# A cross-attention and mixture-of-experts kernel: head loads in three transfers, rank sums taken ahead, a gather that waits, and new orders on every engine

## The chip, the cores and the metric

One core of one Trainium2 chip runs the whole program. The metric is the device time of one execution in microseconds (us), median of the runs. The engines are TensorE (PE, with its weight loads PEld), VectorE (DVE), ScalarE (ACT), GpSimd (POOL) and SyncE (SP, which here only issues transfers). Each takes its own instructions strictly in order, and they meet through semaphores.

## What is computed

Tokens `x` are 4 batches of 256 rows of 256 features, 1024 tokens in all.

```python
def _L0_xattn_ref(teacher_logits, teacher_features, Wq, bq, Wk, bk):
    query = jnp.einsum('bnc,dc->bnd', teacher_features, Wq) + bq
    key = jnp.einsum('bnc,dc->bnd', teacher_features, Wk) + bk
    energy = jnp.einsum('bnd,bmd->bnm', query, key)
    attention = jax.nn.softmax(energy, axis=-1)
    return jnp.einsum('bln,bmn->blm', teacher_logits, attention)

def _L0_ffn_ref(inputs, gate_weight, wi, wo):
    logits = tokens @ gate_weight.T
    probs = jax.nn.softmax(logits, axis=-1)
    top1 = jnp.argmax(logits, axis=-1)
    mask = jax.nn.one_hot(top1, E)
    ranks = jnp.cumsum(mask, axis=0) - 1        # place of a token in its expert
    mask = mask * (ranks < C)                   # C = 160 places per expert
    ...
    dispatch = jnp.einsum('tec,th->ech', sec_mask, tokens)
    hmid = gelu(jnp.einsum('ech,ehi->eci', dispatch, wi))
    eout = jnp.einsum('eci,eih->ech', hmid, wo)
    return jnp.einsum('tec,ech->th', combine_weights, eout)

x = x + _L0_xattn_ref(_layernorm(x), ctx_1024, Wq, bq, Wk, bk)
x = x + _L0_ffn_ref(_layernorm(x), gate_weight, wi, wo)     # 8 experts, 256 -> 1024 -> 256
```

## The kernel before, in words

All matrices are float32. The order on each engine is written out by hand as a list of calls of small functions, one list per engine (PE from L876, DVE from L593, ACT from L409, POOL from L318, SP from L217); a number in brackets is a batch `b` (0 to 3), a tile of 128 tokens `n` (0 to 7) or an expert `e` (0 to 7).

**The front.** `q` and `k` (L787, L796) make queries and keys of the contexts, in three chunks (batch 0, batch 1, batches 2 and 3); the contexts come in three transfers on SP (`context`, L197), the small weights in two on ACT (L361, L362). `en` (L811) makes the energies of a batch, `mx` (L491) their negated maximum on DVE, `exp` (L380) the exponentials on ACT. Tokens stay unnormalised: `bn1`, `st1`, `veps1` (L470 to L483) take their mean and variance, `first_rstd` (L288, POOL) the reciprocal root, `shift` (L485) the product that `shifted_input` (L295, POOL) adds. `turn_by` (L500) scales an identity by the reciprocal of the exponentials' sums; `at` (L818) turns the attention with it and appends the gate's columns; `xm` (L830) multiplies the turned tokens by it, and gives the attended tokens and the gate's logits together. `gate_mean` (L805) and `gate` (L464) take the mean off the gate's weights.

**Routing.** `x1` (L515) makes the new tokens in `rows`, `bn2`, `st2`, `veps2` (L578 to L590) and `second_rstd` (L300, POOL) their statistics. `scaled`, `summed`, `largest`, `less`, `value`, `first`, `chosen` (L520 to L554) make from the logits of a pair of tiles a one-hot `mask` (L553). `forerunners` (L846) and `rk` (L858) count on PE, by small bf16 matmuls, how many earlier tokens went to each expert: for each pair anew in the same 16 columns of PSUM, with one sum per earlier tile. `ranks` and `place` (L556, L562) read the place as a float (for `pick`, L568, which makes the 0/1 matrix of expert 0) and as an integer (for the scatter). `expz` (L394) makes the gate's weight. `scatter` (L306, POOL) writes each tile's rows to a slot table in DRAM, `slots_dram`. Expert 0 doesn't wait for that: `disp` (L865) makes its inputs by matmul from `tok` (L401, ACT) and `onehot`; two copies (L690 on DVE, L437 on ACT) bring them to SBUF.

**The experts.** PE runs `mm1` (L928) and `mm2` (L952) expert by expert. The other experts' rows come back from the slot table once all eight scatters have landed: `got_one` (expert 1), `got_zero` (expert 0, for the end only), `got_main` (experts 2 to 7, 780 KB) and `rest` 0 and 1 (the places 128 to 159 of four experts each). SP issues them (L232 to L236) all but `rest` 0, which ACT issues (L446) behind two GELUs. `load_tile` (L692) normalises a tile on DVE, `dT` (L918) transposes it on PE: tiles 0 and 1 (`got_one`, `rest` 0) inside `mm2(0)`, tile 2 (the first of `got_main`) inside `mm1(1)`, tile 3 ahead of `mm1(2)`. Behind the gathers SP queues four output copies of `rows` (L238), two small gathers (L213) and the weights of experts 3 to 7.

## Time and profile before

| | |
|---|---|
| median of 3 runs | 111.39 us (111.3 to 111.6) |
| the profiled execution's own time | 112.25 us |
| its span | 110.5 us |
| PE busy | 102.0 us, 92% of the span |
| PEld, DVE, ACT, POOL busy | 89.8, 34.6, 31.5, 31.1 us |
| chain that ended last, by engine | PE 78%, DMA 6%, DVE 4%, ACT 4%, issue 3% |
| moved by DMA | 25.77 MB, mean 233 GB/s |

The span runs from the first instruction to the last, the own time has what lies around it. In a timeline, what stands in square brackets behind an instruction is how long its engine had been idle and what ended that. One float32 matmul stands in the trace as two records.

### The profile page before, as it was taken

Reading aid. Unit: us, or ns where it says so; the run is one execution under the profiler, and the core shown is the slowest. Engines: PE = TensorE matmul, PEld = TensorE weight load, DVE = VectorE, ACT = ScalarE, POOL = GpSimd, SP = SyncE. Lnnn points to the kernel's source line nnn. Section 1 sums busy time; section 2 is a strip of 40 time slices with the busy share of each in tenths; the row PEclk is TensorE's granted clock in tenths of the full one; section 3 lists DMA queues with packets and bytes.
Section 4 is the critical chain, followed back from the end, with each engine's and each line's share of the span. In section 5 each row is a group of like instructions: output and inputs, shape, how many; then the busy total and the mean of one; then the engine's idle time right before and its main releaser. Section 6 shows DMA issues by size and latency. Waiting matters only on the chain.

```text
span 110.5 us, 1990 instructions
## 1 busy us (share of the span) xinstructions
PE 102.0 (92%) x758; PEld 89.8 (81%) x758; DVE 34.6 (31%) x151; ACT 31.5 (29%) x81; POOL 31.1 (28%) x55
## 2 busy tenths in 40 slices
PE   5988999999799999999999999999999999999900
PEld 5565888678689989999999998669999999888800
DVE  0019899999930041800420400220020010012110
ACT  3247675367534302332031041002303204100000
POOL 5501388586775000030210210303002011031540
PEclk9999999999999999999999999999999999999995
DMA  2799999999973499999999999950001001001100
GB/s 76 225 336 371 352 296 421 427 415 414 423 278 120 122 279 371 304 309 411 428 424 415 427 421 424 427 190 16 0 0 41 6 0 47 0 0 46 56 3 3
DMA packets 7986, 25.77 MB, mean 233 GB/s; under 512 B 928, under 2 KB 4773, under 8 KB 5928
## 3 DMA queue, kind: packets, MB, share of 16 engines
q1 hardware_dynamic: 6664, 23.24, 56.3%
q0 software_dynamic: 880, 2.12, 5.2%
q10 hardware_dynamic: 432, 0.27, 0.9%
q8 instruction: 6, 0.10, 0.4%
q14 instruction: 4, 0.03, 0.1%
HBM read 21.14 MB, written 4.76 MB: 234 GB/s over the span
## 4 chain that ended last, share of the span: by engine, by line
PE 78%; DMA 6%; DVE 4%; ACT 4%; issue 3%; SPq 1%; POOL 1%; ACTq 0%; DVEq 0%
PE ps L781 71%; DMA shared<-in_ctxT 6%; PE ps L871 3%; ACT shared L406 2%; PE ps L778 2%; PE ps L824 1%; ACT ez L398 1%; DVE rows L516 1%; POOL out L353 1%; SPq L199 1%; DVE nmax L493 1%; ACT attended L366 0%; DVE stats L580 0%; SPq L202 0%; DVE y_end L757 0%
## 5 line engine op out<-in xcount | busy, mean ns | idle before, releaser
L781 PE MATMUL ps<-wo_sb,shared 128*32 128x128 f32 (+2 forms) x320 | 36.6, 337 | 0.0
L781 PE MATMUL ps<-shared,wi_sb 128*128 128x160 f32 x256 | 36.3, 299 | 0.3 <-issue 0.3
L781 PEld LDWEIGHTS ps<-shared,wi_sb 128*128 128x128 f32 x256 | 35.1, 190 | 0.6 <-issue 0.4
L781 PEld LDWEIGHTS ps<-wo_sb,shared 128*32 128x32 f32 (+1 forms) x320 | 29.4, 142 | 5.1 <-issue 1.0
L448 ACT ACTIVATE shared<-ps 128x480 f32<-128x480 f32 (+1 forms) x24 | 12.6, 526 | 48.2 <-PE ps L781 48.2
L346 POOL DMA_INDIRECT out<-y,got x9 | 8.7, 971 | 59.3 <-DVE y L739 44.1
L739 DVE SCALAR_TENSOR_TENSOR y<-ps,share,got 128x256 f32<-128x256 f32 x9 | 4.4, 484 | 48.1 <-PE ps L781 24.7
L314 POOL DMA_INDIRECT slots_dram<-rows,slot x8 | 8.2, 1028 | 4.0 <-issue 1.4
L781 PE MATMUL ps<-attended,shared 128*128 128x272 f32 x32 | 8.4, 402 | 0.2 <-ACT attended L366 0.2
L781 PEld LDWEIGHTS ps<-attended,shared 128*128 128x128 f32 x32 | 5.7, 189 | 1.4 <-ACT attended L366 0.3
L871 PE MATMUL ps<-shared 128*128 128x160 f32 x32 | 5.3, 309 | 0.6 <-ACT shared L406 0.6
L781 PE MATMUL ps<-shared,small 128*128 128x256 f32 (+1 forms) x12 | 5.1, 542 | 0.8 <-DMA shared<-in_ctxT 0.7
L705 DVE TENSOR_SCALAR stok<-got 128x256 f32<-128x256 f32 x7 | 2.7, 415 | 9.0 <-DMA got<-slots_dram 9.0
L871 PEld LDWEIGHTS ps<-shared 128*128 128x128 f32 x32 | 4.6, 190 | 1.0 <-ACT shared L406 0.8
L472 DVE BATCH_NORM_STATS2 stats<-shared 128x6 f32<-128x256 f32 x8 | 3.0, 414 | 6.9 <-DMA shared<-in_x 6.9
L781 PEld LDWEIGHTS ps<-shared,small 128*128 128x128 f32 x12 | 2.4, 230 | 2.8 <-DMA shared<-in_ctxT 1.4
L824 PEld LDWEIGHTS ps<-turner,shared 128*128 128x128 f32 x32 | 4.2, 190 | 0.3
L824 PE MATMUL ps<-turner,shared 128*128 128x136 f32 x32 | 4.4, 279 | 0.0
L384 ACT ACTIVATE shared<-ps,nmax 128x256 f32<-128x256 f32 x8 | 3.7, 469 | 2.0 <-DVE nmax L493 2.0
L297 POOL TENSOR_SCALAR shared<-shared,shift 128x256 f32<-128x256 f32 x8 | 4.0, 508 | 0.4 <-DVE shift L488 0.4
L781 PE MATMUL ps<-shared 128*128 128x256 f32 x16 | 4.0, 384 | 0.0
L366 ACT ACTIVATE attended<-ps 128x264 f32<-128x264 f32 x8 | 3.0, 390 | 3.6 <-PE ps L824 3.5
(82 smaller groups left out, 77.4 us busy)
## 6 DMA issues: line engine op xcount, KB each, us to landing
wi_sb<-in_wi SPq DMA_DIRECT2D x8, 1024.0 KB, 16.6
wo_sb<-in_wo SPq DMA_DIRECT2D x8, 1024.0 KB, 16.7
slots_dram<-fill SPq DMA_DIRECT2D x1, 1300.0 KB, 13.1
shared<-in_x SPq DMA_DIRECT2D x2, 512.0 KB, 7.4
shared<-in_xT SPq DMA_DIRECT2D x2, 512.0 KB, 8.2
out<-rows SPq DMA_DIRECT2D x4, 256.0 KB, 5.4
got<-slots_dram SPq DMA_DIRECT2D x1, 780.0 KB, 6.6
got<-slots_dram SPq DMA_DIRECT2D x4, 130.0 KB, 2.4
```

Of the source, the lines that this page charges most:

```text
L297: nc.gpsimd.tensor_scalar(x_sb[:, n, :], x_sb[:, n, :], 1.0, shift1[:, n:n + 1], ALU.mult, ALU.add).then_inc(xs_done, 1)
L314: nc.gpsimd.indirect_dma_start(slots_dram, bass.IndirectOffsetOnAxis(ap=slot[:, n:n + 1], axis=0), rows[:, n, :], None, bounds_check=last_ ...
L346: nc.gpsimd.indirect_dma_start(out_rows, bass.IndirectOffsetOnAxis(ap=got[:, t, INDEX:INDEX + 1].bitcast(I32), axis=0), y[:, n % 2, :], No ...
L366: return nc.scalar.activation(dst, src, ACT.Copy)
L384: nc.scalar.activation(att[:, b, m, :], p_en[b][:, m * S:(m + 1) * S], ACT.Exp, bias=nmax[:, n:n + 1], accum_out=esum[:, n:n + 1]).then_in ...
L448: nc.scalar.activation(gelu[:, e % RING, a:z, :], p_h[j][:, 0:(z - a) * CAP], ACT.Gelu).then_inc(gelu_done, 1)
L472: nc.vector.bn_stats(stats[:, 0, n, :], x_sb[:, n, :]).then_inc(bn1_done, 1)
L705: nc.vector.tensor_scalar(stok[:, i % 2, :], row[:, 0:H], row[:, MEAN:MEAN + 1], row[:, RSTD:RSTD + 1], ALU.subtract, ALU.mult).then_inc(s ...
L739: nc.vector.scalar_tensor_tensor(y[:, n % 2, :], p_o[n % 2][:, 0:H], share[:, t:t + 1], got[:, t, 0:H], ALU.mult, ALU.add).then_inc(y_done, 1)
L781: return nc.tensor.matmul(dst, lhsT, rhs, start=(k == 0), stop=last)
L824: last = nc.tensor.matmul(p_at[c][:, E + m * P:E + m * P + HALF], att[:, b, m, c * P:(c + 1) * P], turner[:, b % 2, m * HALF:(m + 1) * HAL ...
L871: last = nc.tensor.matmul(p_disp[c], tok[:, n, c * P:(c + 1) * P], onehot[:, n, :], start=(n == 0), stop=(n == NT - 1))
```

## The change

1. **Head loads.** Contexts and small weights lie in one array `head` of 1298 columns and come in three SP transfers: Q's weights, both biases and context 0; K's weights, the gate and context 1; contexts 2 and 3. ACT issues none. `small` now lies inside the buffer `shared`.
2. **Gate mean.** One matmul of 16 columns for two of 8; DVE subtracts the two halves one after the other.
3. **First statistics.** `veps1` and `shift` go from DVE to POOL; tokens are shifted by a subtraction.
4. **Ranks.** All 64 columns (8 tiles by 8 experts) are started once by `rank_base`. After the mask of a pair, `rk` adds its own part and then each tile's sum to the columns of all later tiles. `forerunners` is gone.
5. **Places.** The float and the integer place are made by two calls, `place` and `row_numbers`; a scatter waits for one semaphore per pair, `row_ready`.
6. **Dispatch.** Tile 1 goes first and opens the sums; tile 0 is added on 128 columns. The first group of `mm1(0)` goes by halves: three matmuls on DVE's copy, then three on ACT's.
7. **Gathers.** SP waits for `got_one` and `rest` 0 to land before it issues `got_zero` and all that follows.
8. **Orders.** New lists on PE, DVE, ACT and POOL; `at` is called by half.

```diff
+W_Q, W_BQ, W_BK = 0, C, C + 1
+W_C0 = C + 2
+W_K = W_C0 + S
+W_G = W_K + C
+W_C1 = W_G + HC * E
+W_C2 = W_C1 + S
+W_ROW = W_C2 + 2 * S
+HEAD = [(0, W_K), (W_K, W_C2), (W_C2, W_ROW)]
...
-            context(0)
-            context(1)
+            head(0)
+            head(1)
             inputs(0)
-            context(2)
+            head(2)
...
             sp.wait_ge(scattered, 16 * NT)
             sp.dma_start(got[:, 1, :], by_rank[0:P, 1, :]).then_inc(got_one, 16)
+
+            sp.wait_ge(got_one, 16)
+            sp.wait_ge(rest_here[0], 16)
             sp.dma_start(got[:, 0, :], by_rank[0:P, 0, :]).then_inc(got_zero, 16)
             sp.dma_start(got[:, 2:E, :], by_rank[0:P, 2:E, :]).then_inc(got_main, 16)
...
             def first_rstd(i):
+                four = slice(4 * i, 4 * i + 4)
+                pool.wait_ge(st1_done, i + 1)
+                nc.gpsimd.tensor_scalar(mv[:, four, 1], mv[:, four, 1], EPS, None, ALU.add).then_inc(veps1_done, 1)
                 pool.wait_ge(veps1_done, i + 1)
...
+            def shift(i):
+                pool.wait_ge(rstd1_done, i + 1)
                 four = slice(4 * i, 4 * i + 4)
+                nc.gpsimd.tensor_tensor(shift1[:, four], mv[:, four, 0], rstd1[:, four],
+                                        ALU.mult).then_inc(shift1_done, 1)
...
             def second_rstd(b):
                 pool.wait_ge(veps2_done, b + 1)
+                if b == 0:
+                    pool.wait_ge(filled, 16)
...
             def scatter(n):
-                if n == 0:
-                    pool.wait_ge(slot_done, 1)
-                    pool.wait_ge(zs_done, 2)
-                    pool.wait_ge(filled, 16)
-                elif n % 2 == 0:
-                    pool.wait_ge(zs_done, n + 2)
-                    pool.wait_ge(slot_done, n // 2 + 1)
+
+                if n % 2 == 0:
+                    pool.wait_ge(row_ready[n // 2], 3)
...
-            act.dma_start(small[:, 0:W_FIRST], small_v[:, 0:W_FIRST]).then_inc(small_here[0], 16)
-            act.dma_start(small[:, W_FIRST:W_ROW], small_v[:, W_FIRST:W_ROW]).then_inc(small_here[1], 16)
...
             bn1(0)
-            mx(0)
             bn1(1)
             bn1(2)
+            mx(0)
             gate()
             bn1(3)
+            st1(0)
             recip(0)
             turn_by(0)
-            st1(0)
-            mx(1)
-            veps1(0)
             bn1(4)
             bn1(5)
+            mx(1)
...
-            def forerunners(b):
-
-                if b == 0:
-                    pe.wait_ge(exp_done, 6)
-                    pe.wait_ge(rank_consts, 4)
-                else:
+            def rank_base():
+
+                pe.wait_ge(exp_done, 6)
+                pe.wait_ge(rank_consts, 4)
+                nc.tensor.matmul(p_rank, one_row[:], expert_row[:], start=True, stop=False, skip_group_check=True)
+
+            def rk(b):
+
+
+                pe.wait_ge(mask_done, b + 1)
+                if b:
                     pe.wait_ge(rank_read, b)
-                nc.tensor.matmul(p_rank, one_row[:], expert_row[:], start=True, stop=False, skip_group_check=True)
-                for n in range(2 * b):
-                    nc.tensor.matmul(p_rank, eights[:], mask[:, n // 2, n % 2:n % 2 + 1, :].to_broadcast([P, 2, E]),
-                                     start=False, stop=False, skip_group_check=True)
...
+                last = nc.tensor.matmul(p_rank[:, 2 * b * E:2 * (b + 1) * E], before[:], mask[:, b, :, :], start=False,
+                                        stop=False, skip_group_check=True)
+                for t in range(2):
+                    n = 2 * b + t
+                    if n < NT - 1:
+                        last = nc.tensor.matmul(p_rank[:, (n + 1) * E:], eights[:],
+                                                mask[:, b, t:t + 1, :].to_broadcast([P, NT - 1 - n, E]), start=False,
+                                                stop=True, skip_group_check=True)
+                last.then_inc(rk_done, 1)
...
+                    if e == 0 and j == 0:
+
+
                         for c in range(HC):
-                            last = mm(p_h[j][:, (i - a) * CAP:(i - a + 1) * CAP], wi_sb[:, e, c, i * P:(i + 1) * P],
-                                      dispT[:, c, e, :], c, c == HC - 1)
+                            pe.wait_ge(disp_sb[c], 1)
+                            for i in range(a, z_):
...
```

What the new lists do to the instructions stands here at the three places that the prediction speaks of. DVE at its start, before (L472 is `bn1`, L493 `mx`, L466 `gate`, L498 and L510 the turner, L477 `st1`, L483 `veps1`, L488 `shift`):

```order
L472 BN_STATS stats<-shared 128x6
L493 TENSOR_REDUCE nmax<-ps 128x2
L472 BN_STATS stats<-shared 128x6 x2
L466 TENSOR_TENSOR idg<-small,ps 128x16
L472 BN_STATS stats<-shared 128x6
L498 RECIPROCAL erec<-esum 128x2
L510 TENSOR_SCALAR turner<-idg,erec 128x136 x2
L477 BN_AGGR mv<-stats 128x2 x4
L493 TENSOR_REDUCE nmax<-ps 128x2
L483 TENSOR_SCALAR mv<-mv 128x4
```

and now (L492 `bn1`, L502 `mx`, L484 and L487 `gate`, L497 `st1`, L507 and L519 the turner):

```order
L492 BN_STATS stats<-shared 128x6 x3
L502 TENSOR_REDUCE nmax<-ps 128x2
L484 TENSOR_TENSOR idg<-shared,ps 128x16
L487 TENSOR_TENSOR idg<-idg,ps 128x16
L492 BN_STATS stats<-shared 128x6
L497 BN_AGGR mv<-stats 128x2 x4
L507 RECIPROCAL erec<-esum 128x2
L519 TENSOR_SCALAR turner<-idg,erec 128x136 x2
L492 BN_STATS stats<-shared 128x6 x2
L502 TENSOR_REDUCE nmax<-ps 128x2
```

The first maximum moved behind two statistics, the first aggregation ahead of the turner, the second maximum behind two statistics of the second half. PE around the last two rank groups, before (L871 is `disp`, L853 to L862 the ranks):

```order
L871 MATMUL ps<-shared 128x160 x4
L853 MATMUL ps<-expert_row,one_row 128x16
L855 MATMUL ps<-mask,eights 128x16 x4
L861 MATMUL ps<-mask,before 128x16
L862 MATMUL ps<-mask,eights 128x8
L871 MATMUL ps<-shared 128x160 x4
L853 MATMUL ps<-expert_row,one_row 128x16
L855 MATMUL ps<-mask,eights 128x16 x6
L861 MATMUL ps<-mask,before 128x16
L862 MATMUL ps<-mask,eights 128x8
L871 MATMUL ps<-shared 128x160 x8
```

and now (L885 `disp`, L867 and L872 the ranks):

```order
L885 MATMUL ps<-shared 128x160 x2
L885 MATMUL ps<-shared 128x128 x2
L867 MATMUL ps<-mask,before 128x16
L872 MATMUL ps<-mask,eights 128x24
L872 MATMUL ps<-mask,eights 128x16
L885 MATMUL ps<-shared 128x160 x4
L867 MATMUL ps<-mask,before 128x16
L872 MATMUL ps<-mask,eights 128x8
L885 MATMUL ps<-shared 128x160 x8
```

The seven and nine small matmuls between dispatches became three and two. POOL at the scatters, before (L303 is `second_rstd`, L314 `scatter`):

```order
L314 DMA slots_dram<-rows,slot 1280x260
L303 TENSOR_TENSOR rows<-rows,minus_half 128x2
L314 DMA slots_dram<-rows,slot 1280x260
L303 TENSOR_TENSOR rows<-rows,minus_half 128x2
L314 DMA slots_dram<-rows,slot 1280x260 x2
L303 TENSOR_TENSOR rows<-rows,minus_half 128x2
L314 DMA slots_dram<-rows,slot 1280x260 x4
```

and now (L321, L328):

```order
L328 DMA slots_dram<-rows,slot 1280x260
L321 TENSOR_TENSOR rows<-rows,minus_half 128x2
L328 DMA slots_dram<-rows,slot 1280x260 x3
L321 TENSOR_TENSOR rows<-rows,minus_half 128x2 x2
L328 DMA slots_dram<-rows,slot 1280x260 x4
```

The third and the fourth scatter moved ahead of the third root.

## Rows read from the trace of the kernel before

**Rows 1.** Windows: span, length, busy of PE, PEld, DVE, ACT, POOL, clock, DMA, GB/s

```profile
15.10:20.40 5.30, 5.09 (x32) 4.05 (x30) 5.27 (x25) 3.41 (x15) 4.52 (x8) 1.00 1.02 397
20.40:28.70 8.30, 7.51 (x48) 6.24 (x49) 8.23 (x49) 4.93 (x18) 5.95 (x7) 1.00 1.02 419
28.70:32.40 3.70, 3.69 (x31) 3.33 (x31) 2.51 (x14) 1.30 (x6) 2.55 (x3) 1.00 0.87 355
...
40.00:60.00 20.00, 20.00 (x136) 19.18 (x134) 5.39 (x17) 4.74 (x9) 1.94 (x2) 1.00 1.02 374
```

**Rows 2.** Chain of waits, two pieces: start, length, what

```profile
2.16 6.44 DMA shared<-in_ctxT
...
32.73 7.17 PE ps L781 x44
```

**Rows 3.** Timeline, DVE: start, length, engine, line, operation, out<-in, count, idle before

```profile
7.99 0.43 DVE L472 BATCH_NORM_STATS2 stats<-shared 128x6 f32<-128x256 f32 x1 [6.93 <-DMA shared<-in_x]
8.33 0.67 DVE L493 TENSOR_REDUCE nmax<-ps 128x2 f32<-128x512 f32 x1
...
8.92 0.74 DVE L472 BATCH_NORM_STATS2 stats<-shared 128x6 f32<-128x256 f32 x2
```

**Rows 4.** Timeline, DVE and ACT at the hand-over to the experts

```profile
32.06 0.32 DVE L690 TENSOR_SCALAR shared<-ps 128x160 f32<-128x160 f32 x1 [0.98 <-PE ps L871]
...
32.28 0.30 ACT L437 ACTIVATE shared<-ps 128x160 f32<-128x160 f32 x1 [1.77 <-PE ps L871]
```

**Rows 5.** Timeline, the first gathered rows on ACT's queue, DVE and PE

```profile
36.36 0.57 ACTq L446 DMA_DIRECT2D rest<-slots_dram  x1
...
43.77 0.73 DVE L705 TENSOR_SCALAR stok<-got 128x256 f32<-128x256 f32 x2 [2.92 <-DMA got<-slots_dram]
...
44.30 0.38 PE L778 MATMUL ps<-idg,stok 128*128 128x128 f32 x2
```

**Rows 6.** Timeline, DVE: one add of eps and the instruction behind it

```profile
12.14 0.16 DVE L483 TENSOR_SCALAR mv<-mv 128x4 f32<-128x4 f32 x1
...
12.21 1.40 DVE L472 BATCH_NORM_STATS2 stats<-shared 128x6 f32<-128x256 f32 x4
```

**Rows 7.** Timeline, POOL: two small copies

```profile
9.80 0.33 POOL L285 COPY attended<-idg 128x16 f32<-128x16 f32 x2 [5.58 <-DVE idg L466]
```

**Rows 8.** Timeline, PE: six small sums of the last rank group, then dispatch

```profile
29.53 0.31 PE L855 MATMUL ps<-mask,eights 128*128 128x16 bf16 x6
...
29.75 2.50 PE L871 MATMUL ps<-shared 128*128 128x160 f32 x16
```

**Rows 9.** Timeline, the pick on DVE and the fourth dispatch on PE

```profile
28.02 0.54 DVE L575 TENSOR_SCALAR shared<-first_slots,slot_f,rows 128x160 f32<-128x160 f32 x1
...
28.71 0.78 PE L871 MATMUL ps<-shared 128*128 128x160 f32 x4 [0.61 <-ACT shared L406]
```

**Rows 10.** Timeline, POOL: last reciprocal root and fifth scatter

```profile
28.50 0.73 POOL L303 TENSOR_TENSOR rows<-rows,minus_half 128x2 f32<-128x2 f32 x1
...
29.99 1.04 POOL L314 DMA_INDIRECT slots_dram<-rows,slot  x1 [0.75 <-ACT ez L398]
```

**Rows 11.** DMA issues between 36.3 and 37.4: KB, us from issue to landing

```profile
got<-slots_dram SPq DMA_DIRECT2D x1, 130.0 KB, 2.1
rest<-slots_dram ACTq DMA_DIRECT2D x1, 130.0 KB, 2.8
...
got<-slots_dram SPq DMA_DIRECT2D x1, 780.0 KB, 6.6
```

**Rows 12.** Windows of half a microsecond, columns as in rows 1

```profile
37.50:38.00 0.50, 0.50 (x4) 0.44 (x3) 0.00 (x0) 0.29 (x1) 0.00 (x0) 1.00 0.80 243
...
43.50:44.00 0.50, 0.50 (x6) 0.50 (x5) 0.23 (x1) 0.00 (x0) 0.00 (x0) 1.00 1.20 416
```

**Rows 13.** DMA issue at 43.28, and PE's start of expert 3 in the timeline

```profile
wi_sb<-in_wi SPq DMA_DIRECT2D x1, 1024.0 KB, 8.5
...
54.07 4.51 PE L781 MATMUL ps<-shared,wi_sb 128*128 128x160 f32 x32
```

More of the change, by code:

```diff
@@ L89, in xattn_moe @@
         rows = sb("rows", [P, NT, ROW])
-        small = sb("small", [P, W_ROW])
         idg = sb("idg", [P, 2 * HALF])
@@ L196, in _, with head @@
         def _(sp):
-            def context(i):
-                a, z = CHUNKS[i]
-                sp.dma_start(ctxT[:, a:z, :], ctxT_v[a:z].rearrange("b c s -> c b s")).then_inc(ctx_here[i], 16)
+            def head(i):
+                a, z = HEAD[i]
+                sp.dma_start(small[:, a:z], head_v[:, a:z]).then_inc(head_here[i], 16)
             def inputs(i):
```

301 lines of the change are left out of this document (150 added, 151 removed).

## The prediction

> **What bounds the kernel now.** I read the windows by stage first. From 40 us on PE is busy in every microsecond: 20.00 of 20.00 between 40 and 60 [rows 1], and nothing in the change touches a matmul there. So time can come only from the front (up to the first expert matmul at 32.73 [rows 2]) or from a new wait for rows in the expert part. In the front, between 15.10 and 28.70, DVE is the fullest engine: 5.27 of 5.30 and 8.23 of 8.30, while PE idles 0.21 and 0.79; from 28.70 to 32.40 it is PE, 3.69 of 3.70 [rows 1]. The chain of waits agrees with the start: its first long piece is a context transfer that ends at 8.60 [rows 2]. DVE's own start is its wait for the tokens, 6.93 us up to 7.99 [rows 3].
>
> Second, the timeline at the hand-over. The first expert matmul runs at 32.73; the DVE copy it needs is done at 32.06 + 0.32 = 32.38, the ACT copy at 32.28 + 0.30 = 32.58 [rows 4]. Third, the same timeline at the first gathered rows. Scattering ends so that `rest` 0 is issued at 36.36, and `got_one` with it on SP. The six-expert gather `got_main` is read at 43.77, and the transposes that need it run at 44.30 [rows 5]. DVE's two tiles from it take 0.73 together [rows 5], so the first is there about 0.4 after the landing, near 44.2, and PE takes it at once. **There is next to no slack at this place**, and the change moves exactly this transfer.
>
> I set every later point against M, the first expert matmul (32.73). The transposes of `dT(2)` are due at 44.30 - 32.73 = M + 11.57.
>
> **The change, part by part.** The profiled execution took 112.25 with a span of 110.5; the median of the runs is 111.39, 0.86 lower. I apply the same difference in us to both.
>
> *Head transfers.* The same 649 KB or so go ahead of or beside the same token transfer, in three issues instead of five, and ACT issues none. Q and K may start some tenths earlier, but DVE waits for tokens until 7.99 [rows 3] whatever Q does. Cost 0. If the longer descriptors brought the tokens earlier, all of the DVE-bound front would follow; the nearest row gives no number, and I allow -0.3 to +0.3.
>
> *Order at the start of DVE.* The first maximum moves behind two more token statistics: in the profile it starts at 8.33, and the two statistics then take from 8.92 to 9.66 [rows 3]. The first exponentials and so the first turner come about 0.7 later. But DVE works on without a gap, so its sum is unchanged; the lateness reaches PE only at `at(0)` and again at `at(1)`. I take 0 and keep +0.4 as the bound (half of 0.7 and a little).
>
> *DVE work.* Two adds of eps and two shifts leave DVE. Such an add lasts 0.16 in its row, but the next instruction starts 0.07 later, 12.14 to 12.21 [rows 6], so four save 0.28. The gate gets a second subtraction that waits for the first: 0.15. Net -0.1. POOL gets the four; two small copies there took 0.33 [rows 7], so 0.17 each. They sit in front of the shifted tokens, which `x1` reads some microseconds on; hidden, and 0.2 if not.
>
> *Ranks.* 24 small matmuls become 12. Six took 0.31 [rows 8], so 0.05 each and 0.6 in all. Most of it falls where DVE sets the pace and is worth nothing. The last group does count, because PE is full after it: it has nine matmuls before and two after. Seven at 0.05 would be 0.35, but the six sums start at 29.53 and the dispatch already at 29.75 [rows 8], so they run partly into each other: I take -0.15. The first dispatch drops 32 of 160 columns: 2.50 / 16 = 0.156 per pass [rows 8], times 0.2, times four passes = 0.12, all before the third dispatch, where PE waits anyway. 0.
>
> *Stall at the fourth dispatch.* PE idled 0.61 before 28.71 [rows 9]. The profile names an ACT instruction, but the pick on DVE ended at 28.02 + 0.54 = 28.56, just before it; DVE is what is late. In the new order this pick comes after even more work of the third pair, so the stall moves to the third rank group or the third dispatch rather than going. I count -0.15 of it; the end that reaches furthest is all of PE's idle time up to there, 1.0 [rows 1]. **Front together: -0.4**, between +0.4 and -1.1.
>
> *Hand-over.* The first group of expert 0 now starts after DVE's copy alone and meets ACT's after three matmuls. Gain 32.58 - 32.38 = **-0.2**; between 0 and -0.25.
>
> *Scatter.* The third and fourth scatter go ahead of the third reciprocal root, and the last two roots run together. The last root ran at 28.50, behind a scatter, and the fifth scatter started at 29.99 [rows 10]. The other scatters follow with nothing to wait for, so the end moves with that start, about 0.5 earlier: as much as PE moves. No cost, and none gained, since `rest` 0 is issued by ACT behind its second GELU, at M + 3.6 as before [rows 5].
>
> *The new wait on SP.* `got_zero`, `got_main`, `rest` 1, the output copies and ten weight transfers now queue behind the landing of `got_one` and `rest` 0. These took 2.1 and 2.8 [rows 11]; with less beside them I take 2.4, so SP goes on at M + 6.0 and issues `got_main` at M + 6.45 (0.45 for issuing `got_zero`, a little under ACT's 0.57 [rows 5]). Before, it was issued 6.6 ahead of 43.77 [rows 5, 11], at 37.2 = M + 4.5: it moves back by 2. It took 6.6 to land [rows 11]. For what it takes now, the upper bound is 5.6: of the 390 KB that went ahead of it 260 KB are gone, and at the 243 GB/s of that stretch [rows 12] those took about 1.0. The lower bound is `got_one`'s 2.1 plus the other 650 KB at the best half microsecond near it, 416 GB/s [rows 12]: 1.6, together 3.7. I take the middle, 4.65: landing at M + 11.1, tile at M + 11.57, the very moment PE wants it. I put **+0.1** down, between 0 and +1.0 (with 6.6 unchanged it would be +1.9).
>
> Here the Trainium skill ("DMA: Bandwidth & Descriptors", Anatomy of one DMA, given for transfers from GpSimd) has a rule that does not fit the row: about 2.0 us fixed plus bytes over 436 GB/s per transfer, so 3.8 us for this one where the trace shows 6.6. By the page there would be no stall, and the sum would be 110.8; by the unchanged row it would be 112.7.
>
> The weights behind the wait: the first of them took 8.5 from 43.28, so it was there at 51.8, and it is needed at 54.07 [rows 13]. 2.3 of slack against 1.7 to 2 of delay: hidden, just; if it is not, a few tenths more. The first output scatter waits for the output copies, and has 6 us before anybody needs its buffer.
>
> **Sum:** -0.4 - 0.2 + 0.1 = -0.5: span 110.0, profiled 111.75, median 111.39 - 0.5 = **110.9**.
>
> **The rivals.**
>
> *A, the big gather is late (slower).* Place: `dT(2)`, the transposes at M + 11.57. Each microsecond that `got_main` takes beyond 4.65 is a microsecond of PE. The gain of 0.6 is eaten at 5.15, and the kernel is slower beyond what can be told at 5.5. For: the 6.6 of the row, and the output copies come just as close behind as before. Against: two of the three transfers ahead are gone. At 5.7 the stall is 1.1, and the time 111.39 - 0.6 + 1.1 = 111.9; up to 112.7. Chance 0.27.
>
> *B, the front gets longer.* The later first maximum is paid on PE, and POOL's extra work reaches `x1`: +0.4 for -0.4, the rest as above: 111.39 + 0.4 - 0.2 + 0.1 = 111.7. For: DVE's start is on the path. Against: DVE has work to fill every gap. Chance 0.13.
>
> *C, the orders do more than I credit.* PE's idle time up to 28.7 goes and the last rank group with it: -1.1 - 0.2 + 0.1 = -1.2, 110.2. For: `rk` no longer holds four or six sums between a mask and a dispatch. Against: DVE had 0.1 idle in 13.6 us, so somebody must wait for it. Chance 0.2. That the head transfers do nothing for the end is part of the forecast.
>
> **How the numbers follow.** Forecast 0.40, own range 110.5 to 111.3. A 0.27, B 0.13, C 0.20. The range 110.1 to 112.2 takes in C and most of A, and leaves out a tenth at each end. A measurement of this kernel can tell about 0.3% (0.33 us) from no change. Faster by more: three quarters of the forecast and nearly all of C, 0.49. Slower by more: most of A and over half of B, 0.29. Within: the rest, 0.22.
>
> **What would show it.** In the changed kernel's trace: the two first matmuls of expert 0 about 0.1 behind DVE's copy; DVE still above 95% from 15 us to the last pick; dispatch ending near 31.7; the six-expert gather issued near M + 6.4 and landing near M + 11.1. A gap of PE before the third transposed tile of over 0.5 us makes A right. A first expert matmul later than 32.7 makes B right, one before 31.7 C. The forecast is wrong in kind if a wait ends last that none of these names, such as a weight transfer before expert 3.

## The result, and the profile after

The change made the kernel slower. The median of six runs is 114.58 us (113.93 to 115.37), against 111.61 (111.3 to 112.32) for the kernel before on the same chip: ratio 1.026, with an interval of 1.0222 to 1.0297. Executions more than 1.5% above the fastest of a kernel, as most kernels have some, before too, are left out of the ratios but not of the medians. The profiled execution of after is the fastest of the six, 113.93 with a span of 112.1, and that of before (112.25, span 110.5) lies 0.64 above its median of 111.61. So the two profiles show 1.6 to 1.7 us of the loss, and the medians hold 1.3 more: 0.64 because before's profile lies above its median, 0.65 because after's lies below.

The windows by stage, the last of the front cut at 33.40, where PE now goes idle behind dispatch (32.40 in before) (columns as in [rows 1]):

```profile
15.10:20.40 5.30, 4.80 (x29) 3.51 (x27) 4.59 (x25) 1.80 (x6) 5.30 (x8) 1.00 1.03 394
20.40:28.70 8.30, 5.98 (x35) 5.18 (x35) 6.76 (x41) 4.05 (x16) 7.10 (x8) 1.00 1.01 419
28.70:33.40 4.70, 4.30 (x31) 3.85 (x31) 3.06 (x19) 2.84 (x12) 3.92 (x5) 1.00 0.84 337
40.00:60.00 20.00, 19.87 (x135) 18.82 (x134) 5.81 (x18) 4.30 (x8) 1.95 (x2) 1.00 0.94 326
```

Against [rows 1] two engines have changed places. DVE was full from 15.10 to 28.70 and is now busy 4.59 and 6.76. POOL is the full one: 5.30 of 5.30, then 7.10 of 8.30. The page's list of costly groups names the instruction that filled it. First the group in before, then in after (line, engine, operation, count, then busy us and mean ns):

```profile
L297 POOL TENSOR_SCALAR shared<-shared,shift 128x256 f32<-128x256 f32 x8 | 4.0, 508 | 0.4 <-DVE shift L488 0.4
```

```profile
L313 POOL TENSOR_SCALAR shared<-shared,shift 128x256 f32<-128x256 f32 x8 | 7.4, 935 | 0.1
```

The token shift was written as multiply by 1.0 and add, and is now a single subtraction. One operation instead of two, on the same 128x256 elements, takes 935 ns instead of 508. What that pushes back stands in three timelines of after, POOL, ACT and PE:

```profile
15.70 4.58 POOL L313 TENSOR_SCALAR shared<-shared,shift 128x256 f32<-128x256 f32 x5
20.25 0.72 POOL L321 TENSOR_TENSOR rows<-rows,minus_half 128x2 f32<-128x2 f32 x1
```

```profile
21.07 0.30 ACT L411 ACTIVATE ez<-below,rows 128x8 f32<-128x8 f32 x1 [2.03 <-POOL rows L321]
...
21.66 0.65 ACT L380 ACTIVATE attended<-ps 128x264 f32<-128x264 f32 x2
```

```profile
19.23 1.17 PE L834 MATMUL ps<-turner,shared 128*128 128x136 f32 x8
22.17 0.70 PE L834 MATMUL ps<-turner,shared 128*128 128x136 f32 x4 [1.78 <-ACT attended L380]
22.71 1.08 PE L793 MATMUL ps<-attended,shared 128*128 128x272 f32 x4
```

Five shifts fill POOL up to 20.25. Only then comes the reciprocal root of the first block (`second_rstd(0)`). ACT's exponential of that block's logits (`expz(0)`) waits for it until 21.07. The new order puts `expz(0)` ahead of the copies `at(2)`, which need nothing from POOL. PE needs those copies to free its PSUM for `at(3)`, and stands still for 1.78 us. Dispatch ends later by 0.9 us (30.67 + 2.50 = 33.17, against 29.75 + 2.50 = 32.25 in [rows 8]), and the first expert matmul comes later by 1.2. This is the hand-over, DVE, ACT and PE (before: [rows 2, 4]):

```profile
33.47 0.33 DVE L702 TENSOR_SCALAR shared<-ps 128x160 f32<-128x160 f32 x1 [1.43 <-PE ps L885]
34.19 0.30 ACT L454 ACTIVATE shared<-ps 128x160 f32<-128x160 f32 x1 [2.46 <-PE ps L885]
33.95 1.87 PE L956 MATMUL ps<-shared,wi_sb 128*128 128x160 f32 x12 [0.56 <-issue]
```

M is 33.95 where before had 32.73. The matmul follows DVE's copy by 0.15 (33.80 to 33.95), as meant; it is the copy that starts late, 0.30 behind the end of dispatch. One profile places M no better than within half a microsecond: d3 below, whose front is that of before, has it at 32.19.

The other part of the loss is the moved gather. The chain of waits now runs through it (before: [rows 5, 11]):

```profile
37.49 2.50 DMA rest<-slots_dram
...
40.44 4.88 DMA got<-slots_dram
...
45.34 0.42 DVE stok L717
...
45.81 0.44 PE ps L790 x2
```

`dT(2)` runs at 45.81 = M + 11.86, against M + 11.57: 0.3 us late. So the profiled loss is 1.22 in front of M and 0.29 up to `dT(2)` behind it.

### The profile page after: what moved, and what is told of

The parts are those of the page before. It is cut to its first block, busy times and chain, and to the rows that moved or that the text cites. A ratio compares the mean times of both kernels' runs of the same rounds, so it can differ in the third digit from the quotient of the medians.

```text
span 112.1 us, 1966 instructions
## 1 busy us (share of the span) xinstructions
PE 101.5 (91%) x744; PEld 89.4 (80%) x744; DVE 34.3 (31%) x148; ACT 31.1 (28%) x81; POOL 35.7 (32%) x59
## 4 chain that ended last, share of the span: by engine, by line
PE 63%; DMA 13%; POOL 7%; DVE 7%; issue 3%; SPq 2%; ACT 1%; ACTq 0%
PE ps L793 55%; DMA shared<-in_x 7%; POOL shared L313 5%; DMA got<-slots_dram 4%; PE ps L885 3%; DMA rest<-slots_dram 2%; PE ps L790 2%; PE ps L956 2%; DVE stats L492 1%; DVE rows L525 1%; SPq L204 1%; POOL rstd L303 1%; POOL out L369 1%; DVE stats L592 1%; POOL rows L321 1%
## 5 line engine op out<-in xcount | busy, mean ns | idle before, releaser
L793 PE MATMUL ps<-shared,wi_sb 128*128 128x160 f32 x244 | 34.6, 299 | 0.0
L793 PEld LDWEIGHTS ps<-shared,wi_sb 128*128 128x128 f32 x244 | 33.5, 190 | 0.2
L793 PE MATMUL ps<-shared 128*128 128x256 f32 (+1 forms) x28 | 9.2, 479 | 0.0
L328 POOL DMA_INDIRECT slots_dram<-rows,slot x8 | 8.2, 1023 | 2.0 <-issue 1.6
L793 PEld LDWEIGHTS ps<-shared 128*128 128x128 f32 x28 | 5.7, 226 | 2.3 <-issue 1.7
L313 POOL TENSOR_SCALAR shared<-shared,shift 128x256 f32<-128x256 f32 x8 | 7.4, 935 | 0.1
L885 PE MATMUL ps<-shared 128*128 128x160 f32 (+1 forms) x32 | 5.0, 306 | 0.3 <-DVE shared L587 0.3
L885 PEld LDWEIGHTS ps<-shared 128*128 128x128 f32 x32 | 4.5, 190 | 0.6 <-issue 0.3
L492 DVE BATCH_NORM_STATS2 stats<-shared 128x6 f32<-128x256 f32 x8 | 3.0, 417 | 6.3 <-DMA shared<-in_x 6.3
L525 DVE SCALAR_TENSOR_TENSOR rows<-ps,rstd,shared 128x256 f32<-128x256 f32 x8 | 3.8, 477 | 1.6 <-PE ps L793 1.2
L797 PE MATMUL ps<-warm_w 128*128 128x128 f32 x12 | 2.9, 410 | 1.1 <-DVE warm_w L470 1.1
```

What stands on the lines that cost most here:

```text
L313: nc.gpsimd.tensor_scalar(x_sb[:, n, :], x_sb[:, n, :], shift1[:, n:n + 1], None, ALU.subtract).then_inc(xs_done, 1)
L328: nc.gpsimd.indirect_dma_start(slots_dram, bass.IndirectOffsetOnAxis(ap=slot[:, n:n + 1], axis=0), rows[:, n, :], None, bounds_check=last_ ...
L492: nc.vector.bn_stats(stats[:, 0, n, :], x_sb[:, n, :]).then_inc(bn1_done, 1)
L525: nc.vector.scalar_tensor_tensor(halves(rows[:, n, 0:H]), halves(p_xm[n // 2 % 2][:, n % 2, 0:WIDE])[:, :, E:HALF], rstd1[:, n:n + 1], hal ...
L793: return nc.tensor.matmul(dst, lhsT, rhs, start=(k == 0), stop=last)
L797: nc.tensor.matmul(p_warm[:, 0:P], warm_w[:], warm_w[:], start=True, stop=True)
```

## The experiments

A ratio below is to the kernel before on the same chip. That kernel's median differed by chip: 112.09 beside the a and b runs, 110.8 beside c and d, 111.76 beside e and f. Only ratios are therefore compared across groups. The edits stand here in short: semaphore increments, function names and unchanged arguments are left out.

**Is it the form, and does the new wait cost?** Four kernels.

a1: after with the shift as two operations.

```
-  x_sb[:, n, :], shift1[:, n:n + 1], None, ALU.subtract
+  x_sb[:, n, :], 1.0, shift1[:, n:n + 1], ALU.mult, ALU.subtract
```

> The changed kernel with one edit: POOL's token shift is written with two operations again (times 1, minus the shift) instead of the single subtraction. Theory F (form of the instruction): one such POOL instruction took 935 ns in the changed kernel where the two-operation form took 508 ns; eight of them hold up the first second reciprocal root, which holds ACT through its exponentials of the gate, which stand ahead of the third attention copies, and PE idles 1.78 us. Then the instruction goes back to about 0.5 us, PE's idle time before the third attention falls under 0.4 us, the first expert matmul moves from 33.95 to 32.3 to 32.7, and the time falls by 1.2 to 1.8 us against the changed kernel, to about 113.0. Theory O (orders): the new lists on ACT and DVE are at fault whatever the form; then POOL's instruction stays near 0.9 us (the port is shared with a busier DVE), or it shrinks and the first expert matmul stays within 0.3 us of 33.95.

b1: before with one operation.

```
-  x_sb[:, n, :], 1.0, shift1[:, n:n + 1], ALU.mult, ALU.add
+  x_sb[:, n, :], shift1[:, n:n + 1], None, ALU.add
```

> The kernel before with one edit: POOL's token shift as a single addition of the (negative) shift instead of times 1 plus the shift. Theory F: POOL's instruction grows from 508 to about 930 ns here too. Five of them stand ahead of the first second root, so this root comes about 2 us later, but here ACT has the attention copies of the third batch ahead of the gate's exponentials, so PE is not held the same way; the tokens that the new tokens' sum needs come later, and the time grows by 0.5 to 1.5 us, to 112.1 to 113.1. Theory O: the form costs nothing by itself, the instruction stays near 0.5 us and the time stays within 0.3 us of the kernel before.

a2: after without the new wait.

```
-  sp.wait_ge(got_one, 16)
-  sp.wait_ge(rest_here[0], 16)
```

> The changed kernel without SP's wait for the first two gathers; all else as in the change. Theory W (the wait is the main part of the loss outside the front): the six-expert gather is issued about 3 us earlier relative to the first expert matmul and lands about 1.5 us earlier; the gap before the third transposed tile goes, and the time falls by 0.3 us (the 0.3 us of the profile), to about 114.3; if the wait also explains what the profile doesn't show (the median lies 2.9 us over the kernel before, the profiled span only 1.6 us), it falls by 1.0 or more. Rival: the front alone explains it, and the time stays within 0.3 us of 114.6.

a3: after with the edits of a1 and a2.

```
-  x_sb[:, n, :], shift1[:, n:n + 1], None, ALU.subtract
+  x_sb[:, n, :], 1.0, shift1[:, n:n + 1], ALU.mult, ALU.subtract
-  sp.wait_ge(got_one, 16)
-  sp.wait_ge(rest_here[0], 16)
```

> The changed kernel with both edits: the two-operation token shift and no wait on SP. If the two losses are separate and add up, it falls by 1.5 to 2.5 us against the changed kernel, to 112.1 to 113.1, at the kernel before or up to 1 us over it. If it comes below 111.3, the rest of the change (ranks, hand-over, orders) is worth something; if it stays over 112.5, a further part of the change costs time.

Measured: a1 117.25 (ratio 1.0489, 1.0381 to 1.0596), b1 113.02 (1.0069, 1.003 to 1.0108), a2 117.70 (1.0461, 1.0362 to 1.056), a3 120.99 (1.076, 1.066 to 1.0859). Three of the four (a1, a2, a3) went against what I had written; b1 did not.

The simple theory, that two operations are fast and one is slow, fell with a1: multiply and subtract took 1150 ns each, more than the single subtraction. PE then idled longer, and its clock fell. Windows of a1, then PE's timeline there:

```profile
22.00:23.00 1.00, 0.00 (x0) 0.00 (x0) 0.75 (x5) 0.94 (x6) 1.00 (x1) 1.00 1.04 434
23.00:24.00 1.00, 0.84 (x5) 0.87 (x6) 0.00 (x0) 1.00 (x5) 0.81 (x2) 0.70 1.06 426
24.00:25.00 1.00, 1.00 (x4) 0.77 (x4) 0.00 (x0) 0.75 (x3) 0.97 (x2) 0.50 1.00 418
25.00:26.00 1.00, 1.00 (x4) 0.77 (x3) 0.00 (x0) 0.00 (x0) 0.81 (x2) 0.50 0.96 401
```

```profile
23.16 1.02 PE L834 MATMUL ps<-turner,shared 128*128 128x136 f32 x4 [2.76 <-ACT attended L380]
23.97 2.02 PE L793 MATMUL ps<-attended,shared 128*128 128x272 f32 x4
```

Behind 2.76 us without a matmul the granted clock is 0.50, the 1.2 GHz level, until past 26 us. The four records at 23.97 take 2.02 where the same ones of after take 1.08. A stall is paid there once as waiting and again as matmuls of double length. a2 shows that the pause of after can be enough for it. The code up to there is that of after, the pause has the same 1.78 us, and the clock falls all the same. Windows and PE of a2:

```profile
22.00:23.00 1.00, 0.22 (x1) 0.25 (x2) 1.00 (x10) 1.00 (x6) 0.81 (x2) 0.69 1.06 442
23.00:24.00 1.00, 1.00 (x5) 1.00 (x6) 0.21 (x1) 1.00 (x3) 0.97 (x2) 0.50 0.96 401
```

```profile
22.78 1.02 PE L832 MATMUL ps<-turner,shared 128*128 128x136 f32 x3 [1.78 <-ACT attended L378]
```

From that matmul to the first of the experts it is 13.24 us in a2 (22.78 to 36.02) and 11.78 in after (22.17 to 33.95), so the fall is worth about 1.5 us.

b1 has the slow form in the old order of ACT, and loses 0.7% where after loses 2.6%. POOL, then ACT, in b1:

```profile
16.84 3.69 POOL L297 TENSOR_SCALAR shared<-shared,shift 128x256 f32<-128x256 f32 x4
20.50 0.72 POOL L303 TENSOR_TENSOR rows<-rows,minus_half 128x2 f32<-128x2 f32 x1
```

```profile
17.67 0.79 ACT L366 ACTIVATE attended<-ps 128x264 f32<-128x264 f32 x2 [1.06 <-PE ps L824]
21.32 0.30 ACT L398 ACTIVATE ez<-below,rows 128x8 f32<-128x8 f32 x1 [2.86 <-POOL rows L303]
```

The root is as late as in after (20.50), and ACT waits 2.86 us for it, but the copies `at(2)` had gone ahead at 17.67, and M is 32.74, as in before. Where b1's 0.7% is lost its profile does not show. So most of after's loss needs two things together: the slow shift, and a queue of ACT in which PE's copies stand behind it.

**Taking the two apart.** c1: after with multiply by 1.0 and add, and so the mean negated once for each four tiles.

```
+  nc.gpsimd.tensor_scalar(mv[:, four, 0], mv[:, four, 0], -1.0, None, ALU.mult)
-  x_sb[:, n, :], shift1[:, n:n + 1], None, ALU.subtract
+  x_sb[:, n, :], 1.0, shift1[:, n:n + 1], ALU.mult, ALU.add
```

> After, with the eight token shifts in the form of before (multiply by 1, add the shift) and so the mean negated by one more small POOL operation for each four tiles (about 240 ns each). Theory P (the front is long because POOL's shifts grew from 508 to 935 ns and second_rstd(0), then the logits' exponential, then the copies at(2) stand behind them): the shifts are 508 ns again, second_rstd(0) comes at 17.5 to 18.8 us instead of 20.25, TensorE's idle time of 1.8 us before the third block's attention is gone, first expert matmul at 31.5 to 32.7 (after: 33.95), span 109.5 to 110.9, median 110.5 to 111.7. Rival Q (the new orders of TensorE and VectorE are what lengthens the front, POOL only fills its idle time): second_rstd(0) earlier, but the first expert matmul still after 33.3, time over 113.

c2: after with one line of ACT's order moved.

```
   exp(3)
-  expz(0)
   at(2, 0)
   at(2, 1)
+  expz(0)
```

> After, with one edit of ScalarE's order: the copies at(2,0) and at(2,1) ahead of the exponential of the logits expz(0), as in before; the token shifts stay at 935 ns. Theory P: the copies no longer wait for POOL, so TensorE's 1.8 us of idle before 22.17 goes, but the logits of block 2 still meet a late POOL; first expert matmul 33.0 to 33.7, time 112 to 113.5, granted clock of TensorE at full speed throughout. Rival Q: no change, 114 to 115.

c3: c1 without SyncE's two waits.

```
-  sp.wait_ge(got_one, 16)
-  sp.wait_ge(rest_here[0], 16)
```

> The same kernel as c1_mult_add without SyncE's two waits ahead of the gathers got_zero and got_main. If the wait helps on its own (it helped after by 3 us: 117.70 against 114.58), this is slower than c1_mult_add by 2 to 3 us, with rest0 landing 4 to 6 us after its issue and TensorE waiting over 2 us before 47 us. If the wait helped only because the front was late, it is within 0.5 us of c1_mult_add.

c4: before with the three head transfers alone (with the constants, the packed input and PE's waits that go with them).

```
-  context(0)
-  context(1)
+  head(0)
+  head(1)
   inputs(0)
-  context(2)
+  head(2)
...
-  act.dma_start(small[:, 0:W_FIRST], small_v[:, 0:W_FIRST])
-  act.dma_start(small[:, W_FIRST:W_ROW], small_v[:, W_FIRST:W_ROW])
```

> Before, with the contexts and small weights in the three transfers of after, and nothing else of the change. As recorded for the prediction: 0 with 0.4 either way. By what after's profile shows (first token statistics at 6.67 instead of 7.99 us): the front starts 0.5 to 1.3 us earlier, and if no engine's order holds it back the first expert matmul comes at 31.7 to 32.5 (before: 32.73) and the time is 110.3 to 111.3; if the tuned orders absorb it, 111.3 to 111.9.

c1: 111.27, ratio 1.0026 (0.9995 to 1.0057). c2: 111.88, 1.0101 (1.0066 to 1.0136). Either mends most of the 2.6%, so the way is shown from both ends. In c1 a shift lasts 470 ns and the root comes at 18.26. In c2 the shifts still last 937 ns, but ACT and PE read:

```profile
19.92 0.85 ACT L380 ACTIVATE attended<-ps 128x264 f32<-128x264 f32 x2 [0.98 <-PE ps L834]
20.96 0.30 ACT L411 ACTIVATE ez<-below,rows 128x8 f32<-128x8 f32 x1 [0.19 <-POOL rows L321]
```

```profile
20.46 0.73 PE L834 MATMUL ps<-turner,shared 128*128 128x136 f32 x4 [0.19 <-DVE turner L519]
```

The first expert matmul comes at 32.27 in c1 and at 32.58 in c2. The second is earlier than I expected of c2 (33.0 to 33.7). Counted from DVE's first maximum (at 7.66, 7.76 and 7.34 in after, c1 and c2), the front takes 26.3 us in after, 24.5 in c1 and 25.2 in c2.

c4: 110.89, 1.0003 (0.9984 to 1.0022). The head transfers are worth nothing at the end. In c4's DVE timeline the first token statistics start at 6.60 (7.99 in [rows 3]). That looks like a gain and is none: d3, with the transfers of before, has them at 6.55. They start at 6.55 to 7.99 in the five profiles with the old transfers and at 6.01 to 7.55 in those with the new, so the executions differ here and not the kernels. PE waits for the third head transfer until 8.14, DVE's second maximum waits for PE. First c4, then d3:

```profile
6.60 0.43 DVE L474 BATCH_NORM_STATS2 stats<-shared 128x6 f32<-128x256 f32 x1 [5.54 <-DMA shared<-in_x]
...
11.03 0.69 DVE L495 TENSOR_REDUCE nmax<-ps 128x2 f32<-128x512 f32 x1 [0.98 <-PE ps L783]
```

```profile
6.55 0.43 DVE L474 BATCH_NORM_STATS2 stats<-shared 128x6 f32<-128x256 f32 x1 [5.49 <-DMA shared<-in_x]
```

c3's four runs took 110.16, 114.56, 114.83 and 115.71 us. They lie too far apart for a ratio. The last is the profiled one. `rest` 0 is issued on ACT's queue at 35.63, `got_main` on SP's at 36.09, and `rest` 0 does not land until 42:

```profile
35.63 0.56 ACTq L462 DMA_DIRECT2D rest<-slots_dram  x1
```

```profile
42.02 0.41 DVE L716 TENSOR_SCALAR stok<-rest 128x256 f32<-128x256 f32 x1 [4.22 <-DMA rest<-slots_dram]
```

```profile
42.49 0.44 PE L789 MATMUL ps<-idg,stok 128*128 128x128 f32 x2 [3.01 <-DVE stok L716]
```

```profile
42.00:43.00 1.00, 0.51 (x3) 0.47 (x4) 0.78 (x3) 0.00 (x0) 0.00 (x0) 0.96 1.08 380
43.00:44.00 1.00, 1.00 (x4) 0.78 (x3) 1.00 (x4) 0.00 (x0) 0.00 (x0) 0.50 1.18 349
```

It took 6.4 us for the 130 KB that took 2.8 in before [rows 11], where `rest` 0 went out at 36.36 and `got_main` at 37.2. In this run PE pays twice again: 3.01 us of waiting, then a stretch at 0.50. The runs of 114.56 and 114.83 had a mean granted clock of 1.00, so their loss came without such a stretch; they were not profiled. The same is why a2 and a3 lost by dropping the wait: there `rest` 0 took 6.8 and 6.1 us to land, and PE waited 3.42 and 2.70 us for it. In both it was issued just behind `got_main` (39.57 against 39.53, 40.47 against 40.36).

**What the wait costs, and whether the order of issue can replace it.**

d1: c1 without the waits, `rest` 0 issued by SyncE instead of ACT.

```
   sp.dma_start(got[:, 1, :], by_rank[0:P, 1, :])
+  sp.dma_start(rest[:, 0, :], by_rank[P:CAP, 0:PER_STACK, :])
-  sp.wait_ge(got_one, 16)
-  sp.wait_ge(rest_here[0], 16)
   sp.dma_start(got[:, 0, :], by_rank[0:P, 0, :])
   sp.dma_start(got[:, 2:E, :], by_rank[0:P, 2:E, :])
```

> c1_mult_add without SyncE's two waits, and rest0 issued by SyncE right behind got_one (ahead of got_zero and got_main) instead of by ScalarE. Theory R (rest0 lands late only where it is issued less than half a microsecond ahead of got_main: 35.63 against 36.09 in c3_mult_add_no_wait, landing 6.4 us after; 36.4 against 37.2 in before, landing 2.8 us after): rest0 starts about 35.6 and lands within 3.2 us although got_main follows about 0.9 us later, got_main lands before TensorE asks for it, no time of TensorE's is lost before dT(1) or dT(2), span 109.0 to 109.5, median 110.4 to 111.1 (c1_mult_add: 111.27), never 114. Rival S (any gather beside got_main is slow, only a finished rest0 helps): rest0 lands 5 to 6.5 us after its issue, TensorE waits 2 to 3 us, 114 or more.

d2: c4 with the hand-over by halves.

```
-  if e == 0:
-      pe.wait_ge(disp_sb, 2)
+  if e == 0 and j == 0:
+      for c in range(HC):
+          pe.wait_ge(disp_sb[c], 1)
+          for i in range(a, z_):
```

> c4_head_alone with the hand-over of after (the first group of matmuls with the two halves on semaphores of their own). As predicted for the hand-over: 0.2 us less, from the 0.26 to 0.47 us between the last dispatch matmul and the first expert matmul; ratio to before 0.997 to 0.999. If the second copy (ScalarE's) is what the six matmuls of the second half then wait for, no gain: 1.000.

d3: before with the two waits alone.

```
   sp.dma_start(got[:, 1, :], by_rank[0:P, 1, :])
+  sp.wait_ge(got_one, 16)
+  sp.wait_ge(rest_here[0], 16)
   sp.dma_start(got[:, 0, :], by_rank[0:P, 0, :])
```

> Before with SyncE's two waits ahead of got_zero and got_main, and nothing else of the change. By what was predicted (got_main 0.1 us late at dT(2)) 1.001; by what after and c1_mult_add show (0.25 to 0.3 us of stall), 1.001 to 1.004. The runs of before that lie some 2.3 us above the others (3 of 24 on the last chip, 112.9 to 113.1) should be gone if they come from rest0 landing beside got_main; if they stay, they come from elsewhere.

d4: d1 with c2's edit of ACT's order.

```
   exp(3)
-  expz(0)
   at(2, 0)
   at(2, 1)
+  expz(0)
```

> d1_rest_on_sync with ScalarE's copies at(2) ahead of expz(0). POOL is no longer late in d1, so the order should matter little: within 0.3 us of d1_rest_on_sync. If it is faster by more, ScalarE's order still costs time in c1_mult_add; if both it and d1 lie below before, the change's other parts are worth having.

d1: 110.94, 1.0012 (0.9988 to 1.0036). `rest` 0 goes out at 35.59 and `got_main` at 36.87, 1.3 us apart, and `rest` 0 is in DVE's hands at 38.31. None of the ten runs reaches 112. So a `got_main` under way beside it does not by itself make `rest` 0 late. Whether the wider gap did it or the shared queue is not separated; before had two queues and a gap of 0.8 us, and did not have the delay either. Nor is the gap to `got_main` separated from the place beside `got_zero`: wherever `rest` 0 was late (a2, a3, c3) it was issued behind `got_zero`, wherever it was not, at least 0.36 us ahead of it. Against c1 (1.0026), which has the wait, the gain is within the intervals.

d2: 110.53, 0.9964 (0.9944 to 0.9984). The copy of DVE ends at 31.85 and the first expert matmul runs at 31.99, 0.14 later, where [rows 2, 4] have 0.35. That is the 0.2 us predicted, and it is measured inside one profile. But `dT(2)` then runs at M + 11.77, where c4 has M + 11.58, so in these two profiles 0.2 us of lead is gone again by there.

d3: 111.67, 1.0071 (1.0031 to 1.011). In the kernel before, the wait costs 0.8 us (0.3 to 1.2), not 0.1. Chain of d3:

```profile
38.91 5.03 DMA got<-slots_dram
43.96 0.42 DVE stok L707
...
44.43 0.44 PE ps L780 x2
```

M is 32.19 there, so `dT(2)` runs at M + 12.24. Of what I asked about single runs: d3 has one at 113.39 with the wait and e1 one at 114.78 with `rest` 0 on SP, so they do not all come from `rest` 0 landing beside `got_main`.

d4: 111.66, 1.0082 (1.0051 to 1.0113). c2's edit, which gained 1.6% on the slow shifts, loses 0.7% on the fast ones. Its profile has ACT's `expz` and `token` on the chain before dispatch, and the first expert matmul at 32.69 (d1: 32.12); but DVE's first maximum is 0.58 later too (8.27 against 7.69), so the profile does not show where the 0.7% goes. The better order of this queue depends on the durations of the shifts.

**What the rest of the change is worth.**

e1: d2 with `rest` 0 on SyncE.

```
   sp.dma_start(got[:, 1, :], by_rank[0:P, 1, :])
+  sp.dma_start(rest[:, 0, :], by_rank[P:CAP, 0:PER_STACK, :])
...
-  act.dma_start(rest[:, 0, :], by_rank[P:CAP, 0:PER_STACK, :])
```

> d2_head_handover (before with the three head transfers and the hand-over by halves) with rest0 issued by SyncE behind got_one. d2's profile shows no TensorE wait for the gathers, so nothing should be gained at the median: 0.995 to 0.998 of before. If the runs 2.3 us above the others (2 of 10 in d2) come from rest0 landing beside got_main, there are none here; if they stay, they come from elsewhere.

e2: before with the rank sums alone (`rank_base`, the new `rk`, `p_rank` of 64 columns).

```
-  forerunners(0)
+  rank_base()
...
-  forerunners(1)
...
-  forerunners(2)
...
-  forerunners(3)
```

> Before with the rank sums of after alone (one row of PSUM for all blocks, each mask added once for every later tile; no other order changed). As recorded: about 0.15 us less from the 0.24 us of six small matmuls behind the sixth dispatch, ratio 0.998 to 0.999. Rival: the sums now stand behind the mask, so VectorE's ranks come later by the additional matmuls: 1.000 to 1.003.

e3: after with the subtraction first.

```
-  x_sb[:, n, :], shift1[:, n:n + 1], None, ALU.subtract
+  x_sb[:, n, :], shift1[:, n:n + 1], 1.0, ALU.subtract, ALU.mult
```

> After with the token shift as (x - shift) * 1.0, two operations with the subtraction first. If GpSimd has one fast form, multiply then add: 900 to 1200 ns each and 114 to 117.5 in all. If it is a second operation other than a subtraction that makes it fast: about 500 ns each and 111 to 112 (c1_mult_add: 470 ns, 111.27).

e4: e1 with the edit of e2.

> e1_head_handover_rest with the rank sums of e2. If the three terms add up as recorded (hand-over 0.2, ranks 0.15), 0.994 to 0.997 of before. Against d1_rest_on_sync (1.0012), which has these parts and the new orders of all engines, the leaner gate mean and the first block's work on POOL besides, the difference is what those orders cost or give: if e4 is below 0.998, they give back 0.3 us or more.

f1: e4 with `rest` 0 on ACT again, which undoes the edit of e1.

> e4_all_kept with rest0 issued by ScalarE again, as in before. If e4 lost its gain because rest0 stood ahead of got_main on SyncE's queue (got_main issued at 36.80, landed 6.5 us later, dT(2) at 43.80 although the first expert matmul came at 31.16): got_one and rest0 both at about 35.2, got_main issued 0.85 us behind got_one (about 36.0), landed by 42.7, dT(2) at 43.0 to 43.4, ratio to before 0.989 to 0.995. If the parts themselves do not add up: the same as e4, 1.002 to 1.007.

f2: before with the edits of d2 and e2, without the head transfers.

> Before with the hand-over by halves and the rank sums, head transfers as in before. If the three head transfers add nothing at the end (c4_head_alone: 1.0003): the same as f1 within 0.2%. Otherwise f1 is ahead by up to 0.5 us.

| | median | ratio | interval |
|---|---|---|---|
| e1 | 112.70 | 1.0087 | 1.0052 to 1.0123 |
| e2 | 111.59 | 0.9971 | 0.9951 to 0.9991 |
| e3 | 117.31 | 1.051 | 1.0464 to 1.0556 |
| e4 | 112.07 | 1.0045 | 1.0014 to 1.0076 |
| f1 | 111.60 | 0.9977 | 0.9952 to 1.0001 |
| f2 | 111.79 | 0.9996 | 0.9971 to 1.0022 |

e3 settles the form. Its shift, against c1's:

```profile
L313 POOL TENSOR_SCALAR shared<-shared,shift 128x256 f32<-128x256 f32 x8 | 9.2, 1156 | 0.2
```

```profile
L314 POOL TENSOR_SCALAR shared<-shared,shift 128x256 f32<-128x256 f32 x8 | 3.7, 470 | 0.1
```

e2 gives the rank sums 0.3% (0.1 to 0.5), where I had written 0.1 to 0.2. e1 and e4 missed: `rest` 0 ahead of the others on SP pushes `got_main` back, which PE waits for 0.36 us in e1 and 0.59 in e4. e1 lies 1.2% above d2, which is more than that; the rest is not found. In e4 the first expert matmul is at 31.16, the earliest of all, and yet the chain reads:

```profile
36.80 6.51 DMA got<-slots_dram
43.31 0.03 issue
43.34 0.42 DVE stok L705
43.76 0.04 issue
43.80 0.44 PE ps L778 x2
```

43.80 is M + 12.64: the expert part no longer follows PE but the end of the scatters. f1 with `rest` 0 back on ACT issues `got_main` at 36.57 and has `dT(2)` behind PE's own work, without a wait; its ratio is 0.7% below e4's. But f1 is not better than e2 or d2 alone, so the gains do not add up. I expected 0.989 to 0.995. f2 says the same without the head transfers: it lies within 0.2% of f1, as expected if those add nothing, and its interval does not reach the 0.6% that d2 and e2 promise together.

Why is not settled, but two things can be read. f1's first expert matmul comes at 31.70, half a microsecond after e4's with the same front; DVE's first maximum is 0.56 later too (7.58 against 7.02), so that is again the start of the execution. And the gathers do not come earlier with M. `got_one` goes out at M + 3.61 in c4, M + 3.86 in d2 and M + 4.02 in f1, behind the last scatter. PE's four records of `dT(0)` and `dT(1)` take 0.60 us in c4, 0.67 in d2 and 0.79 in f1, where a wait of 0.2 for `rest` 0 stands. `dT(2)` runs at M + 11.76 in f1. So some of what is gained ahead of M is lost again at `rest` 0. d2 and e2 are the only versions below both kernels beyond their intervals, each by 0.3 to 0.4%, and f2, with the edits of both, is not.

## Why the prediction was wrong

Forecast 110.9, range 110.1 to 112.2; measured 114.58. Term by term:

- **The token shift, priced at nothing.** This is the step that failed. The part on DVE work counts the small instructions that POOL "gets", calls them "hidden, and 0.2 if not", and has no line at all for the eight large ones whose form was changed. They took 935 ns instead of 508. The changed kernel stands at 1.026 and c1 at 1.0026: 2.3%, 2.6 us. The row of before could price the old form and no row could price the new one, so it needed bounds and got nothing.
- **Queues past which a step is moved.** `expz(0)` ahead of `at(2)` on ACT was not looked at, although it makes PE wait for POOL. c2 puts it at 1.6% with the slow shifts. It is not a second loss on top of the 2.3%, but the way by which they reach PE. Rival B had the place ("POOL's extra work reaches x1") and the size at +0.4. `x1(1)` did wait for POOL, but only 0.4 us; the large wait was elsewhere. By my own signs B came true (a first expert matmul later than 32.7, here 33.95), and DVE, which I wanted above 95%, was busy 87% and 81% in the two stretches. In before POOL was busy 4.52 of 5.30 and 5.95 of 8.30 [rows 1], and I had read those numbers for DVE and PE only.
- **The wait on SP, +0.1.** Right in its steps, too small in its sum. `got_main` was issued at M + 6.49 in after (predicted M + 6.45). Its landing took 4.88, 4.69, 5.49, 5.03, 4.5 and 4.93 in after, c1, c2, d3, a1 and e3, against 4.65 taken: 4.9 in the mean, inside my bounds. `dT(2)` was 0.25 to 0.9 behind M + 11.57 in the first four, and d3 makes it 0.8 us in all. "Next to no slack at this place" was right, and so every tenth above 4.65 was paid. By the estimate from the Trainium skill ("DMA: Bandwidth & Descriptors", Anatomy of one DMA) it would have been 3.8; the shortest here was 4.5. What I missed is that the wait also buys something: without it, with the orders as they are now and `rest` 0 on ACT, `rest` 0 lands 6 us or more after its issue (a2, a3, c3).
- **Head transfers, 0.** Right: c4 is 1.0003. The tokens that seem to come 1.3 us earlier in the profiles of after and c4 come as early in d3 with the old transfers.
- **Hand-over, -0.2.** Right where it was priced: 0.14 instead of 0.35 between DVE's copy and the matmul in d2, 0.15 in after. At the end of the kernel f2 leaves it open. What I had no term for is that in after the copy itself starts 0.30 behind the modelled end of dispatch, where c1's starts 0.24 ahead of it (31.80 against 32.04). It costs about 0.5 us. a1 and e3 have it too, c1 and c2 do not, with the same code there; no view names a cause, and it stays open.
- **Ranks, -0.15.** Right in its sign: e2 alone is 0.3% faster (0.1 to 0.5). Together with the hand-over, in f2, nothing is left of either that can be told from no change.
- **Front -0.4 in all.** c1 keeps everything but the form and stands at 1.0026, of which d3 gives the wait 0.0071. What is left is -0.0045, or -0.5 us, where the recorded terms without the wait make -0.6. The two intervals together leave about 0.5 us of doubt on it.

With these terms the sum is -0.5 + 0.8 + 2.6 = +2.9 for the measured 2.97, but that is no test of it: 2.6 is after less c1, and -0.5 is what d3 leaves of c1. The profiles show 1.7 of the 2.97 between them; the rest is where they lie among their runs. It is tempting to put after's slower runs down to a clock that fell behind the 1.78 us of idle, as in a2. Their mean granted clocks speak against it. About 3.4 us at 0.50, as in a1 and a2, would take 0.015 off the mean of a span of 112 us (an estimate: 3.4 x 0.5 / 112). The runs of 114.3, 114.45 and 115.37 us had 0.997, 0.999 and 0.995 and leave no room for it; only that of 115.36, at 0.973, looks like such a fall. What else separates after's median from its profiled run, 0.65 us, stays open.

## What to carry to other kernels

Price every instruction whose operands or operations change, even if it looks like less work; where no row has the new form, bound it by the nearest ones, and try it alone first. Before moving a step in an engine's queue, list which slower engine it waits for and who waits for what now stands behind it. And where a small and a large gather go out from two queues within half a microsecond of each other, or the small one behind, the small one can take twice as long to land. Look at the times of issue before a wait between them is dropped, and count the wait as what it prevents as well as what it costs. Last, before a difference between two profiles is read as an effect, look whether a third kernel without the change has it too.
